# Attention gathers: GpSimd waits at every second quad of tiles until its own rows have landed

## What is computed

```python
# layer 2, for each of 3 sub-layers l            (8 heads of 32)
q_dst = Q[dst]
kt = typed(K[src], W_E[l], edge_type)
scores = sum(q_dst * kt, -1) / scale * mu[l].T[edge_type]
m = segment_max(scores, dst)
e = exp(scores - m[dst])
w = e / (segment_sum(e, dst)[dst] + 1e-10)
agg = segment_sum(V[src] * w[..., None], dst)     # then Wo, layer norm, MLP, layer norm
# layer 3
alpha = a_src . h[src] + a_dst . h[dst] + sum(relu(edge_attr @ edge_W.T + edge_b) * h[dst], -1)
alpha = where(alpha >= 0, alpha, 0.2 * alpha)     # then the same softmax over dst and sum of h[src]
```

## Time and profile before

| | us |
|---|---|
| median of 3 executions | 6562.15 (6557.18 to 6564.07) |
| the profiled execution's own time | 6555.16 |
| its span, first to last instruction | 6553.4 |
| TensorE busy (19341 matmuls) | 4457.6 (68%) |
| VectorE busy | 3838.9 (59%) |
| GpSimd busy | 3397.7 (52%) |
| ScalarE busy | 1599.6 (24%) |
| DMA queue of GpSimd (software_dynamic) | 549.90 MB, 34.6% of 16 engines |
| DMA queue of SyncE (hardware_dynamic) | 404.91 MB, 19.2% of 16 engines |

### The profile page before, as it was taken

The page is one execution under the profiler, slowest core; times in us unless marked ns, Lnnn a source line. Parts: engine busy times, 40 slices in busy tenths (PEclk is TensorE's granted clock), DMA queues, the critical chain, the costliest instruction groups (busy, mean ns, idle before and its releaser), DMA issues. The chain is left out here.

```text
span 6553.4 us, 68667 instructions
## 1 busy us (share of the span) xinstructions
PE 4457.6 (68%) x19341; PEld 3500.4 (53%) x19341; DVE 3838.9 (59%) x8689; ACT 1599.6 (24%) x3857; POOL 3397.7 (52%) x3109
## 2 busy tenths in 40 slices
PE   5566664567776566667966676698566678856676
PEld 4444443534445455556855555587455557745554
DVE  7544442544445466776337776743576675667777
ACT  3333332200003221122422221144121123412221
POOL 2577788066663556550355555314555550066663
PEclk9777887778888788778987777799777889978888
DMA  3577777345565656553145555513655562066665
GB/s 137 112 114 115 115 116 101 105 157 188 182 176 156 195 181 183 179 173 72 66 153 180 179 178 176 138 38 110 184 177 177 179 163 61 25 195 196 187 196 142
DMA packets 495905, 959.74 MB, mean 146 GB/s; under 512 B 84453, under 2 KB 296627, under 8 KB 491010
## 3 DMA queue, kind: packets, MB, share of 16 engines
q0 software_dynamic: 224512, 549.90, 34.6%
q1 hardware_dynamic: 270898, 404.91, 19.2%
q10 hardware_dynamic: 128, 0.52, 0.0%
HBM read 718.56 MB, written 236.50 MB: 146 GB/s over the span
## 5 line engine op out<-in xcount | busy, mean ns | idle before, releaser
L1446 POOL DMA_INDIRECT L2a_rows<-kv_rows,typed_index x960 | 971.2, 1012 | 610.5 <-DVE L2a_weighted L1601 332.6
L1751 PE MATMUL L2a_sums<-L2a_weighted,L2a_hot 128*128 128x264 f32 x2784 | 844.0, 456 | 164.7 <-DVE L2a_weighted L1601 160.3
L865 POOL DMA_INDIRECT sum_rows<-L0s_rows,L0s_row_of x464 | 731.5, 1576 | 200.3 <-issue 132.0
L1740 PE MATMUL L2a_query<-x,L2a_turned 128*128 x2784 | 781.8, 431 | 43.8 <-ACT L2a_turned L1695 25.6
L1751 PEld LDWEIGHTS L2a_sums<-L2a_weighted,L2a_hot 128*128 128x128 f32 x2784 | 602.2, 225 | 313.7 <-DVE L2a_weighted L1601 187.3
L1740 PEld LDWEIGHTS L2a_query<-x,L2a_turned 128*128 128x128 f32 x2784 | 604.4, 221 | 161.0 <-issue 51.2
L1446 POOL DMA_INDIRECT hold<-kv_rows,typed_index x432 | 446.8, 1034 | 428.2 <-DVE L2a_weighted L1601 263.4
L1271 POOL DMA_INDIRECT L1s_rows<-rows,index x464 | 450.7, 971 | 382.1 <-ACTq L87 161.5
L1446 POOL DMA_INDIRECT L3a_rows<-feature_rows,index x464 | 493.1, 1063 | 272.4 <-issue 146.3
L1703 ACT ACTIVATE L2a_hot<-L2a_hot 128x512 f32<-128x512 uint8 x348 | 218.7, 629 | 1399.1 <-PE L2a_sums L1751 682.5
L1001 PE MATMUL L0s_message<-features,L0s_share 128*128 x928 | 323.8, 510 | 336.8 <-ACT L0s_share L966 336.8
(11 more groups left out here) (415 smaller groups left out, 8907.4 us busy)
## 6 DMA issues: line engine op xcount, KB each, us to landing
code_rows<-L1s_code SPq DMA_DIRECT2D x116, 512.0 KB
L3a_code<-code_rows SPq DMA_DIRECT2D x116, 512.0 KB
L0s_wide<-source_rows SPq DMA_DIRECT2D x29, 1024.0 KB, 7.5
L2a_turn<-turned_rows SPq DMA_DIRECT2D x87, 256.0 KB
L2a_pens<-mask_rows SPq DMA_DIRECT2D x87, 256.0 KB
L2a_hot<-hot_rows SPq DMA_DIRECT2D x87, 256.0 KB
kv_rows<-L2d_key_rows SPq DMA_DIRECT2D x50, 384.0 KB, 2.6
kv_rows<-L2d_value_rows SPq DMA_DIRECT2D x150, 128.0 KB, 2.4
```

What stands on the lines that cost most here:

```text
L865: pool.indirect_dma_start(c.sum_rows[u], bass.IndirectOffsetOnAxis(ap=row_of[:, 4 * n + u:4 * n + u + 1], axis=0), rows[n % ring][:, u, :] ...
L1446: pool.indirect_dma_start(rows[n % ring][:, u, :], None, table, bass.IndirectOffsetOnAxis(ap=index_of[:, t:t + 1], axis=0)).then_inc(lande ...
L1740: last = pe.matmul(query[q % 2][:, u, :], turned[quad % 2][:, u, :], at(c.q, b[2 * q + u // 2]), start=True, stop=True)
L1751: last = pe.matmul(sums[(m * WP + j) % held][:, :], hot[quad % 2][:, j % 2 * 2 + k, :], weighted[:, 2 * j + k, :], start=k == 0, stop=k == 1)
```

## The change

From the third quad on, at every even quad n, GpSimd waits after the ring wait until the four gathers of quad n - 1 have landed: its semaphore must have reached 64 for each use of the buffer so far. The wait is met at n = 2, 4, ..., 114, that is 57 times in each of the four attentions. No instruction is moved, no DMA added.

```diff
@@ -1441,6 +1441,8 @@
         def _(pool):
             for n in range(WG * WQ):
                 wait(pool, weighted_ready, n - ring + 1)
+                if n and n % 2 == 0:
+                    pool.wait_ge(landed[(n - 1) % ring], 64 * ((n - 1) // ring + 1))
                 for u in range(4):
                     t = n * 4 + u
                     pool.indirect_dma_start(rows[n % ring][:, u, :], None, table,
```

## The result

The changed kernel takes 6647.02 us (median of 4, 6643.41 to 6654.69), beside 6563.11 us of the kernel before on the same chip: a ratio of 1.0131, 95% interval 1.0113 to 1.0148. It is 1.3% slower. The forecast was 6519 us, range 6420 to 6640; the rival "dear landings" had 6629 us.

A forecast was written before the change was run, and what follows sets the result against it. Bound by a cycle of gather burst, held TensorE semaphore, `pick`, `weigh` and ring wait; pauses break it. L2a -83 us, L3a +40, sum -43: 6555.16 to 6512 us, plus 7 for the median: 6519 us, range 6420 to 6640.

The forecast's parts named there:

- dear landings: Rival: SyncE's loads share the DMA engines and slow landings; 3.35 us extra a pause, 6629 us; chance 0.22.
- What bounds the kernel: Long gather streams hold back TensorE's semaphore, so `pick`, `weigh` and ring wait form a cycle, 27.8 us a group in L2a.
- No relief: Rival: late semaphores have another cause or 8 gathers are still too many; the cycle stays, 6824 us; chance 0.08.
- no effect: Rival: pauses fall into time GpSimd waits anyway or come back in an earlier `pick`; 6562 us; chance 0.08.
- The sum: Gathers, gaps, pauses and last landing added: L2a gains 83 us in three attentions, L3a loses 40, together -43 us.
- The wait as an instruction costs nothing that I can see: At GpSimd's even quads: the added wait lies in the 0.30 us gap that is there anyway.
- Landing itself: Pause from a quad's last gather to its landing: 3.15 us, 2.85 over the gap, for L2a and L3a.
- The tails: L2a's slow pauses at quads 112 and 114, near an attention's end: 6.6 us each, 6.3 over the gap.
- its sum of 6440 us: Kernel time if landing follows the skill page, 2.6 us for 262 KB; about 78 us below the forecast's sum.
- point of decision: Pause length over the gap at which the gain is gone: 3.05 us, over 220 ordinary pauses.
- The prediction's own sign of being wrong: Several-us "remote" waits before `pick`, GpSimd still waiting for `weigh`, or DMA waits below 2.4 or above 3.4 us.
- L3a: Last attention: 126.1 us of ring waits go, as many pauses come; 812.8 us against 773.1, a loss of 40.

The follow-up runs named there:

- c1_one_wait: The changed kernel with each even quad's ring wait taken one quad earlier, so the gather behind a pause has one wait: 6504.42 us, 0.9915 of the kernel before.
- b1_before: The kernel before, unchanged, run again for its profile on another chip of the slower kind: 6562.14 us, ratio 0.9999.
- b2_after: The changed kernel, unchanged, run again on another chip of the slower kind: 6638.82 us, 1.0121 of the kernel before.
- a1_l2a: The change in L2a only, no pauses in L3a, on a chip where the kernel before took 5753.59 us: 6326.97 us, 1.1009 of the kernel before.
- c2_old: The changed kernel waiting for quad n - 2 instead of n - 1, so two waits but no pause: 6554.25 us, 0.9991 of the kernel before.

## Why the prediction was wrong

**What bounds the kernel** was read rightly for the chip whose trace it was: on it, and on H1 and H2, two full pauses a group bring `pick` in time (36, 51 and 10 us of waits, for 400), and the ring waits vanish. In the group of the earlier trace rows the trace has the semaphore of `expand` rise at 2649.55, 7.3 us behind the end of its row and 0.02 us before `pick`: it was late, and VectorE was not. "No relief" and "no effect" are out. That L2a's time is unchanged is a balance, since in c1_one_wait, with 0.5 us less a pause, its gathers take 776 to 784 us instead of 807 to 809. One reading of the earlier trace rows was wrong and without effect: TensorE, 545.10 us busy, was not busy for less time than GpSimd (472.67).

The Trainium skill's rule (page "SBUF — State Buffer", section "Who interferes with whom") that a DMA never contends with a compute engine holds for Q1 as far as its trace shows, with no late `pick` beside 464 gathers in 630 us. The rule stands in a section on SBUF's ports. On the held chips b1_before (`pick` waits 398 us) and b2_after (51 us with the pauses) show that VectorE does get TensorE's result late while gathers stream; so the prediction was right not to follow the rule to "no relief". Which part of the chip holds the semaphore, a port or something else, no run shows.

**The sum.** The step that failed is the price of the pause: "The wait as an instruction costs nothing that I can see". In the order in which the change writes its two waits, it costs 0.48 us from quad 10 on, because the landing is met last and its wait is written last. That is 25 us of each attention in L2a and 25 in L3a, 101 us in all. The pauses took more than the sum had in both kinds of attention:

| us | forecast | after | c1_one_wait |
|---|---|---|---|
| L2a (first attention): 57 pauses | 186.5 | 217.1 | 196.6 |
| the 464 gathers themselves | 472.7 | 461.2 | 455.5 |
| from first to last gather | 781.0 | 806.7 | 775.8 |
| L3a: 57 pauses | 189.9 | 241.6 | 240.3 |
| the 464 gathers themselves | 493.2 | 495.0 | 453.1 |
| from first to last gather | 804.9 | 861.8 | 817.1 |

(The rest are gaps between gathers, 122 us in the sum and 124 to 128 measured.) From first to last gather the three attentions of L2a are 25.7, 28.0 and 27.5 us over the sum and L3a 56.9, together 138 us; the 6512 us forecast for the profiled execution and its 6648.61 differ by 137.

With a single wait, c1_one_wait came to 0.9915 of before, where the forecast was 0.9934. That is close partly by luck: its pauses were longer than forecast, by 10 us in L2a's first attention and by 50 us in L3a, and its gathers were shorter by 17 and 40 us. Why they were shorter is told at the end.

**Landing itself** was sized well in L2a and too small in L3a. Quads 4 to 8 of the first attention took 3.01, 3.01 and 2.95 us, of which 0.26 us lie between the semaphore's rise and the gather. Over an attention's 55 ordinary pauses the landing alone, from the end of the last gather's row to that rise, took 2.97 to 3.09 us in L2a and 3.42 us in L3a; the sum had 2.88 us for both, which is its 3.15 less the 0.27 us that GpSimd itself needs. The tails (6.6 us forecast) were 7.55 and 7.3 us in the first attention, 0.48 us of each through the order. The estimate by the Trainium skill (page "DMA: Bandwidth & Descriptors", section "Anatomy of one DMA — SWDGE (gpsimd) path"), 2.6 us, is under the 2.75, 2.75 and 2.69 us that landing took at quads 4 to 8, by 0.1 to 0.15 us, and its sum of 6440 us is 200 us off.

**Dear landings** was the rival that came true in its size (6629 us) and in its point of decision (3.05 us over the gap; measured 3.4 in L2a and 3.8 in L3a, tails aside), but only half by its reason. In L2a nearly all of the excess is the order of the waits, which no rival named. In L3a landing was dear as well, and by place: 3.74 us at the first quads of a group and 3.03 us at the third ones. In the time from 4 us before such a landing began to its end, SyncE's queue moved 1.3 MB at the first and 0.5 MB at the third quads, which fits its code loads as the reason; no run took the loads away, so this stays argued. The prediction's own sign of being wrong, waits above 3.4 us, was there (3.83 and 4.24).

**L3a** was forecast to lose 40 us and lost 96. Its ring waits, 126.1 us, went as forecast; its pauses cost 52 us more than the sum had.

## What to carry to other kernels

A pause that breaks a harmful stream must be priced with everything that follows its semaphore: its length times its number, once the engine that pauses is the bound. Give it only where the stream does harm (one full pause in the middle of each burst gave 0.971 on H3, two short ones a group in L2a 0.962 on H1 but, with the other order, 0.987 on H3; two full ones a group, L3a included, 1.013), and write the wait that is met last first. And a stall that the profile can only call "remote" may belong to the chip: run the kernel before on another one before tuning against it, since all six versions that ran on the quick chips lost, by 5 to 10%.

## What the runs showed of the hardware that was not expected

- The same kernel takes 5752 to 5754 us on two chips and 6560 to 6610 us on three others and in the result, 14 to 15% above, at equal times of single gathers (L3a: 488.9 and 493.1 us for 464). In L3a the difference is 752 to 630 us, and `pick` waits 53 us on the one and 1.8 us on the other. A layer without a softmax shows it too: layer 1's 464 gathers span 671 us in the trace of before and 600 us in a1_l2a. Layer 0 does not (its gathers span 919 and 921 us), and TensorE's granted clock over the first 1150 us is 0.80 in both. What differs between the chips was not found.
- The order of two waits on GpSimd's gather is worth 0.48 us when the wait written last is the one that is met last, and nothing when both are met or the one met last is written first (c2_old).
- In L3a the gathers themselves got shorter with the better order or a single wait, at pauses of the same length (240.3 us in 57 in c1_one_wait, 241.6 after the change). The page's groups of the two kernels:

```profile
L1448 POOL DMA_INDIRECT L3a_rows<-feature_rows,index x464 | 495.0, 1067 | 380.6 <-DMA L3a_rows<-feature_rows,index 241.6
```

```profile
L1449 POOL DMA_INDIRECT L3a_rows<-feature_rows,index x464 | 453.1, 977 | 377.6 <-DMA L3a_rows<-feature_rows,index 240.3
```

42 us came from there. Some gathers take 1.5 to 2.0 us instead of 0.95, 58 of them in L3a after the change and 2 in c1_one_wait. What doubles them shows in the timeline of the kernel before, in the group of the earlier trace rows:

```profile
2627.43 1.21 DVE L1601 TENSOR_TENSOR L2a_weighted<-L2a_rows,L2a_weighted 128x1024 f32<-128x1024 f32 x1
2627.56 1.90 POOL L1446 DMA_INDIRECT L2a_rows<-kv_rows,typed_index  x1 [0.30 <-issue]
```

The gather starts 0.13 us behind the start of a `weigh` and ends 0.82 us behind its end. In the trace after the change all 104 long gathers of the four attentions start 0.05 to 0.52 us behind the start of a `weigh` and end 0.82 to 0.85 us behind its end, and all 101 gathers that start 0.03 to 0.48 us behind one are long. So a gather that starts just behind a `weigh` seems to wait for its end; half a microsecond in the pause changes which gathers do.
